# A layer's head in two parts of TensorE, and the experts' rows fetched ahead of a phase border

## What is computed

```python
x = x + _L0_attn_ref(_layernorm(x), ...) + _L0_ffn_ref(...)   # a selective state-space block; FP4 linear layers
x = x + _L1_attn_ref(...) + _L1_ffn_ref(...)                  # gated delta rule; mixture of 8 experts
x = x + _L2_attn_ref(...) + _L2_ffn_ref(...)                  # local attention; gated linear layers
x = x + _L3_attn_ref(...) + _L3_ffn_ref(...)                  # linear attention; gated linear layers
```

```python
uc = silu(conv(u))
dbc = uc @ W_x                       # 256 -> 8 + 16 + 16 columns
dt_r, Bs, Cs = dbc[..., :8], dbc[..., 8:24], dbc[..., 24:]
dt = softplus(dt_r @ W_dt + b_dt)    # 8 -> 256 columns
# then, token by token: h = h * exp(dt * A) + (dt * u) * B;  y = sum over states of h * C
```

## Time and profile before

| what | value |
|---|---|
| median of three runs | 637.83 us (636.1 to 640.2) |
| the profiled execution | 636.67 us, its span 635.0 us |
| TensorE matmul busy | 566.0 us (89%) |
| VectorE busy | 452.7 us (71%) |
| ScalarE busy | 385.8 us (61%) |
| GpSimd busy | 360.9 us (57%) |
| mean granted clock of TensorE | 0.97 of full speed |

### The profile page before, as it was taken

How to read it: one execution, slowest core, us unless ns; L and a number is a source line. 1 busy time by engine, 2 the same in 40 slices (tenths; PEclk the granted TensorE clock), 3 DMA queues, 4 the chain that set the end, 5 groups by cost and what they waited for, 6 DMA issues and landing times. The chain is left out here.

```text
span 635.0 us, 10717 instructions
## 1 busy us (share of the span) xinstructions
PE 566.0 (89%) x3813; PEld 456.0 (72%) x3813; DVE 452.7 (71%) x798; ACT 385.8 (61%) x751; POOL 360.9 (57%) x306
## 2 busy tenths in 40 slices
PE   5999978899999999898887989798999868989997
PEld 2444578799998998576654956798788756776766
DVE  6799798999999986995575797243333575648662
ACT  4679799779979794565459677222211234748670
POOL 0578778988899884688610840864801650224430
PEclk9999699899999999899898999898999999999999
DMA  5035033334434511100350011612412110000002
GB/s 130 4 79 96 13 88 71 84 99 107 112 96 105 100 68 38 39 1 1 88 141 2 2 18 24 160 42 79 131 31 64 39 30 0 1 2 1 2 1 67
DMA packets 43230, 35.77 MB, mean 56 GB/s; under 512 B 11895, under 2 KB 32297, under 8 KB 43178
## 3 DMA queue, kind: packets, MB, share of 16 engines
q1 hardware_dynamic: 42154, 32.99, 21.1%
q0 software_dynamic: 1024, 2.10, 1.1%
HBM read 28.98 MB, written 6.09 MB: 55 GB/s over the span
## 5 line engine op out<-in xcount | busy, mean ns | idle before, releaser
L891 DVE TENSOR_TENSOR_SCAN l0s_ring<-l_XM,l0s_ring,bank 128x512 f32<-128x512 f32 x96 | 114.5, 1259 | 5.3 <-ACT l_XM L602 4.4
L602 ACT ACTIVATE l_XM<-l_DT,l_negA 128x512 f32<-128x512 f32 x120 | 79.7, 712 | 10.2 <-DVE l0s_ring L891 10.0
L749 POOL TENSOR_TENSOR l0s_ring<-l0s_ring,l0s_c_rest 128x1024 f32<-128x1024 f32 x32 | 65.8, 2056 | 18.3 <-DVE l0s_ring L891 9.1
L749 POOL TENSOR_TENSOR l0s_ring<-l0s_ring,all_XF 128x1024 f32<-128x1024 f32 x31 | 66.4, 2146 | 7.9 <-DVE l0s_ring L891 5.5
L449 PE MATMUL bank<-all_ident,l0s_ring 128*128 128x128 f32 x512 | 66.7, 275 | 0.0
L449 PEld LDWEIGHTS bank<-all_ident,l0s_ring 128*128 128x128 f32 x512 | 58.7, 142 | 0.0
L2050 POOL DMA_INDIRECT all_XNT<-gy,all_slot x16 | 15.5, 971 | 37.0 <-DMA gy<-l1s_ys 31.2
L418 PE MATMUL bank<-all_ident,all_XNT 128*128 128x128 f32 x256 | 34.0, 275 | 1.0 <-DVE l0s_ring L891 0.7
L332 PE MATMUL bank<-l_XM,l_wins 128*128 128x512 f32 x64 | 31.8, 642 | 0.9 <-ACT l_XM L546 0.9
L625 ACT ACTIVATE all_XNT<-all_OUTF,l_wins 128x256 f32<-128x256 f32 x72 | 30.5, 495 | 0.2
L418 PEld LDWEIGHTS bank<-all_ident,all_XNT 128*128 128x128 f32 x256 | 29.1, 142 | 2.0 <-DVE l0s_ring L891 0.9
(11 more groups left out here) (452 smaller groups left out, 1594.9 us busy)
## 6 DMA issues: line engine op xcount, KB each, us to landing
l0s_c_rest<-bc_rows SPq DMA_DIRECT2D x16, 512.0 KB, 5.1
all_XF<-bc_rows SPq DMA_DIRECT2D x16, 512.0 KB, 4.9
l_wall<-in_L_ffn_W SPq DMA_DIRECT2D x14, 256.0 KB, 4.6
all_X<-in_L_attn_x SPq DMA_DIRECT2D x4, 256.0 KB, 3.7
gx<-l1m_TD SPq DMA_DIRECT2D x1, 1024.0 KB, 5.2
gy<-l1m_TD SPq DMA_DIRECT2D x1, 1024.0 KB, 8.6
out<-all_X SPq DMA_DIRECT2D x4, 256.0 KB, 3.3
gy<-l1s_ys SPq DMA_DIRECT2D x7, 128.0 KB, 1.8
```

What stands on the lines that cost most here:

```text
L602: nc.scalar.activation(dst, DT[:, j, block_of(n)], ACT.Exp, scale=negA[:, j, n % DS:n % DS + 1]).then_inc(decay_ready, 1)
L749: nc.gpsimd.tensor_tensor(hc[n % CRING][:, :, :], h(n)[:, :, :], wide(c_wide[p % HRING][:, n % 2, :]), ALU.mult).then_inc(hc_ready, 1)
L891: nc.vector.tensor_tensor_scan(h(n)[:, j, :], factor, added, before, ALU.mult, ALU.add).then_inc(h_ready, 1)
```

## The change

**Head of layer 0.** Each block of 512 tokens is cut into two halves of 256, g = 0 and 1. `project` writes half g to partitions 64g to 64g + 39 of bank 4: four matmuls of 256 columns, alternating between the two sets of output columns of the array. `keep_dbc` copies each half by itself, and `DBC` and `wdt` hold half g from partition 64g on. `step_size` is four matmuls of 256 columns with 8 rows each, alternating between rows 0 to 7 and rows 64 to 71 of the array; the first two go to different banks, and the third and fourth each wait until the matmul that wrote their bank before is complete. `spread` is two matmuls of 256 columns, the second waiting for the first; `turn_b` turns the 8 tiles of half 0, waits, and turns those of half 1. `store` is two transfers a block, and `wdt` is loaded twice.

**Layer 1.** `fetch_rows` moves from the head of phase l1s to the end of SP's list in phase l1m; it still waits for the whole scatter. In l1s SP starts with the weights of experts 5 to 7, and `wo` gets a counter of its own. On TensorE, ScalarE and VectorE `experts()` comes first, without the waits for the two chunks, and all 16 chunks follow.

```diff
@@ -154,12 +155,12 @@
         DTU = big.sb("DTU", [P, JT, T])
-        DBC = big.sb("DBC", [DR + 2 * DS, T])
+        DBC = big.sb("DBC", [2 * HALF + DR + 2 * DS - HALF, T // 2])
         win = big.sb("win", [P, 2 * DI])
...
         wx = big.sb("wx", [P, JT, DR + 2 * DS])
-        wdt = big.sb("wdt", [DR, DI])
+        wdt = big.sb("wdt", [HALF + DR, DI])
         wout = big.sb("wout", [P, JT, P])
@@ -256,6 +257,8 @@
             block_of = lambda n: blk(n // DS)
+            half = lambda b, g: slice(b * BLK + g * HBLK, b * BLK + (g + 1) * HBLK)
+            dbc = lambda g, rows, b: DBC[g * HALF:g * HALF + rows, bass.ts(b, HBLK)]
             zy = lambda b, i: ZT[:, (JT * b + i) * BLK:(JT * b + i + 1) * BLK]
@@ -264,13 +267,14 @@
                         sp.wait_ge(dbc_ready, b + 1)
-                        sp.dma_start(bc_rows[:, blk(b)], DBC[DR:DR + 2 * DS, blk(b)]).then_inc(bc_stored[b], 16)
+                        for g in range(2):
+                            sp.dma_start(bc_rows[:, half(b, g)], DBC[g * HALF + DR:g * HALF + DR + 2 * DS, bass.ts(b, HBLK)]).then_inc(bc_stored[b], 16)
 
...
                         if 2 * p % DS == 0:
-                            sp.wait_ge(bc_stored[2 * p // DS], 16)
+                            sp.wait_ge(bc_stored[2 * p // DS], 32)
                         s, at = DS + 2 * p % DS, p % HRING
@@ -289,7 +293,8 @@
                     sp.dma_start(wx[:, :, :], W["L0_attn_W_x"].rearrange("(j p) c -> p j c", p=P)).then_inc(proj_loaded, 16)
-                    sp.dma_start(wdt[:, :], W["L0_attn_W_dt"]).then_inc(proj_loaded, 16)
+                    for g in range(2):
+                        sp.dma_start(wdt[g * HALF:g * HALF + DR, :], W["L0_attn_W_dt"]).then_inc(proj_loaded, 16)
                     sp.wait_ge(zeroed, 2)
@@ -345,19 +350,24 @@
                         pe.wait_ge(u_ready, JT * (b + 1))
-                        pe.wait_ge(proj_loaded, 96)
+                        pe.wait_ge(proj_loaded, 112)
                         if b:
...
                         for j in range(JT):
-                            last = nc.tensor.matmul(S.bank[4][0:DR + 2 * DS, :], wx[:, j, :], UC[:, j, blk(b)], start=(j == 0), stop=(j == JT - 1))
+                            for g in range(2):
+                                last = nc.tensor.matmul(S.bank[4][g * HALF:g * HALF + DR + 2 * DS, 0:HBLK], wx[:, j, :], UC[:, j, half(b, g)],
+                                                        start=(j == 0), stop=(j == JT - 1))
                         last.then_inc(dbc_done, 1)
...
                         pe.wait_ge(dbc_ready, b + 1)
-                        for j in range(JT):
-                            if b:
-                                pe.wait_ge(max_ready, JT * (b - 1) + j + 1)
-                            nc.tensor.matmul(S.bank[6 + j][:, :], wdt[:, j * P:(j + 1) * P], DBC[0:DR, blk(b)], start=True, stop=True).then_inc(dt_done, 1)
+                        if b:
+                            pe.wait_ge(max_ready, JT * b)
+                        for i, (j, g) in enumerate(((0, 0), (1, 1), (0, 1), (1, 0))):
+                            if i >= 2:
+                                pe.wait_ge(dt_done, 2 * JT * b + i - 1)
+                            nc.tensor.matmul(S.bank[6 + j][:, g * HBLK:(g + 1) * HBLK], wdt[g * HALF:g * HALF + DR, j * P:(j + 1) * P], dbc(g, DR, b),
+                                             start=True, stop=True).then_inc(dt_done, 1)
 
@@ -374,20 +384,31 @@
                     def spread(n):
-                        row = S.ident[0:DR + 2 * DS, DR + n % DS:DR + n % DS + 1].broadcast_to([DR + 2 * DS, P])
                         if n == 0:
...
                             pe.wait_ge(dtu_kept, 2 * (n // DS + 1))
-                        nc.tensor.matmul(bank_b[:, :], row, DBC[:, block_of(n)], start=True, stop=True).then_inc(b_spread, 1)
+                        for g in range(2):
+                            if g:
+                                pe.wait_ge(b_spread, 2 * number(n) + 1)
+                            at = g * HALF
+                            row = S.ident[at:at + DR + 2 * DS, at + DR + n % DS:at + DR + n % DS + 1].broadcast_to([DR + 2 * DS, P])
+                            nc.tensor.matmul(bank_b[:, g * HBLK:(g + 1) * HBLK], row, dbc(g, DR + 2 * DS, n // DS), start=True, stop=True).then_inc(b_spread, 1)
 
...
                         pe.wait_ge(w_copied, 3)
-                        for t in range(TILES):
-                            last = nc.tensor.transpose(bank_t[:, t * BC:(t + 1) * BC], DBC[0:BC, bass.ts(t, P)], S.ident[0:BC, 0:BC])
-                        last.then_inc(b_turned, 1)
+                        for g in range(2):
+                            if g:
+                                pe.wait_ge(b_turned, 1)
+                            at = g * HALF
+                            for b in range(NBLK):
+                                for k in range(2):
+                                    t = b * TPB + 2 * g + k
+                                    last = nc.tensor.transpose(bank_t[:, t * BC:(t + 1) * BC], DBC[at:at + BC, b * HBLK + k * P:b * HBLK + (k + 1) * P],
+                                                               S.ident[at:at + BC, at:at + BC])
+                            last.then_inc(b_turned, 1)
 
...
@@ -559,11 +580,13 @@
                         act.wait_ge(dbc_done, b + 1)
-                        nc.scalar.activation(DBC[:, blk(b)], S.bank[4][0:DR + 2 * DS, :], ACT.Copy).then_inc(dbc_ready, 1)
+                        for g in range(2):
+                            last = nc.scalar.activation(dbc(g, DR + 2 * DS, b), S.bank[4][g * HALF:g * HALF + DR + 2 * DS, 0:HBLK], ACT.Copy)
+                        last.then_inc(dbc_ready, 1)
 
...
                         for j in range(JT):
-                            act.wait_ge(dt_done, JT * b + j + 1)
+                            act.wait_ge(dt_done, 2 * JT * b + JT + j + 1)
                             nc.scalar.activation(DTU[:, j, blk(b)], S.bank[6 + j][:, :], ACT.Abs, bias=b_dt[j]).then_inc(abs_ready, 1)
...
@@ -861,7 +884,7 @@
                     def input_of(n):
-                        dve.wait_ge(b_spread, number(n) + 1)
+                        dve.wait_ge(b_spread, 2 * number(n) + 2)
                         if n // DS < 2:
...
@@ -1351,6 +1373,7 @@
                         sp.wait_ge(tt_ready, 32 * NSUB)
+                        fetch_rows(sp, S, E)
 
...
@@ -2021,8 +2044,9 @@
                     def _(sp):
-                        sp.dma_start(wo[:, :], W["L1_attn_Wo"]).then_inc(loaded, 16)
-                        fetch_rows(sp, S, W, E)
+                        for e in range(EARLY + 1, NE):
+                            fetch_expert(sp, W, E, e)
+                        sp.dma_start(wo[:, :], W["L1_attn_Wo"]).then_inc(wo_loaded, 16)
                         for i, n in enumerate("qkv"):
@@ -2172,12 +2196,6 @@
                         def experts():
-                            pe.wait_ge(u_ready, BEFORE)
-                            pe.wait_ge(ut_ready, BEFORE)
-                            pe.wait_ge(st_new, BEFORE)
-                            pe.wait_ge(ss_new, BEFORE - 1)
-                            pe.wait_ge(p_ready, BEFORE)
-                            pe.wait_ge(og_ready, BEFORE)
                             pe.wait_ge(E.rows_loaded, 16 * (2 + SLOTS // P - TILES))
...
@@ -2410,25 +2428,15 @@
 
+                        experts()
                         pe.wait_ge(zeroed, 1)
-                        for c in range(BEFORE):
+                        for c in range(CH):
                             carry(c)
...
                             if c:
-                                outputs(c - 1)
-                        products(BEFORE - 1)
-                        outputs(BEFORE - 1)
-                        experts()
-                        for c in range(BEFORE, CH):
-                            carry(c)
-                            turn_state(c)
-                            if c > BEFORE:
-                                products(c - 1)
-                            states(c)
-                            if c > BEFORE:
                                 outputs(c - 1)
@@ -2770,26 +2776,17 @@
                         nc.vector.tensor_copy(identb[:, :], S.ident[:, :]).then_inc(identb_made, 1)
+                        experts()
                         dve.wait_ge(zeroed, 1)
-                        for c in range(BEFORE):
+                        for c in range(CH):
                             copy_state(c)
                             if c:
-                                products(c - 1)
-                            states(c)
-                            if c:
-                                outputs(c - 1)
-                        products(BEFORE - 1)
-                        outputs(BEFORE - 1)
-                        experts()
-                        for c in range(BEFORE, CH):
-                            copy_state(c)
-                            if c > BEFORE:
```

(6 more changed lines are left out.)

14 lines of the change are left out of this document (7 added, 7 removed).

## The result

The changed kernel takes 633.31 us (median of 22 runs, 630.44 to 638.54), the kernel before 636.15 us (22 runs, 634.13 to 640.37): ratio 0.9958, 95% interval 0.9941 to 0.9975. That is inside the range of the forecast. But the gain is 2.8 us and not 6.3: that the time itself lies only 1.8 us above the forecast's 631.5 is because the kernel before came out 1.7 us faster here than in its three first runs (637.83). The profiled execution took 632.66 us with a span of 630.9 us, against 636.67 and 635.0.

What follows compares the result with a forecast made beforehand. TensorE was taken to bound the head, with VectorE idle before its first input, and the rows' late fetch the border. Head 2.8 plus border 3.5 gave 6.3 us: 637.83 - 6.3 = 631.5 us, range 628.5 to 636.0.

Steps and rivals of the forecast that it cites:

- Projection: Layer 0 head: eight steps of 0.215 us take the time of five, 1.07 us, gaining 0.65 us a block.
- the engine takes records in their order: Projection on TensorE: half 0's second record waits for its first and only runs beside half 1's first; hence five steps.
- The rival of full overlap: Layer 0 head: each pair of matmuls costs half; total gain 7.4 us, 630.4 us; chance 0.14.
- Step sizes: Layer 0 head: both waits for earlier matmuls are covered, all ends at 1.29 us, gaining 0.43 us.
- ScalarE as the bound: Layer 0 head: ScalarE limits two periods to shrinking 1.03 and 0.62 us; fourth keep_dbc 3.4 us earlier, head gives 2.8.
- A start of the scans that is earlier by x brings everything behind it forward by x: From the scans' start to their end VectorE is nearly never idle, so the lead carries on, less first-step losses; 2.8 us.
- a danger of the clock inside the head: Rival: half clock from first step sizes (29 us) to 66 us loses 18 us, giving 650 us; chance 0.06.
- Fetch of the rows: Before phase l1s: SP's longer list is hidden by 1.9 us; the experts' first transpose comes 7.1 to 7.35 us earlier.
- a sign of being wrong: Border before l1s: the prediction is wrong if the rows come more than 1 us behind it.
- The clock at the border: Rival: a half-clock stretch of 3.4 us falls on the experts, half is lost; gain 4.6, 633.2 us; chance 0.16.
- Two chunks at 3.6 us: Behind the experts: two more recurrence chunks cost 2 x 1.79 = 3.6 us, leaving 3.5 us net from the border.
- 3.6 us more room: Gather of results: starts 7.1 us earlier while chunk 8 comes 3.5 us earlier, so it gets 3.6 us more.

Runs made afterwards that it cites:

- the grouped order: Changed kernel with the projection's matmuls ordered half 0 / j 0, half 0 / j 1, half 1 / j 0, half 1 / j 1: one run, 627.63 us.
- the single copy: Changed kernel with one keep_dbc copy of 104 partitions in place of two of 40, W_x padded with zero columns: 629.77 us, ratio 0.9910.
- the delay: Kernel before with the head's edits, plus seven scratch multiplications on VectorE ahead of the first scan input: 642.41 us, ratio 1.0111.
- e_after3: The changed kernel, nothing else altered, run again on the third chip: 626.52 us (6 runs), ratio 0.9888.

## Why the prediction was right or wrong

**Projection: the step that failed is "the engine takes records in their order".** I made five half-steps of it, a gain of 0.65 us. It is four: a gain of 0.86 us a block, and the grouped order shows that the premise was wrong and not only the count. The rival of full overlap was right here.

**Step sizes: right, for another reason.** 1.42 us, a gain of 0.49 where 0.43 was forecast. With full overlap the gain should have been 0.86; the third matmul's wait for the first was called covered, and is not: the second pair starts 0.75 us behind the first (29.33 and 28.58), where two steps take 0.43. The wait costs 0.3 us.

**ScalarE as the bound: right.** It has no idle time in front of the last `keep_dbc`, which is 3.8 us earlier (3.4 forecast), because TensorE's larger gain counts up to the second block. The two copies take 0.77 us, 0.72 forecast. The first input comes 3.3 us earlier (3.0 forecast) and nothing is lost behind it: 3.23 us are there at the end of the scans, where I had 2.8. The way from the first `keep_dbc` to the first input is 41.2 us in all five traces without the head's edits and 37.9 in all six with them (without the single copy and the delay).

**"A start of the scans that is earlier by x brings everything behind it forward by x": failed, for the most part by the granted clock.** Without the head's edits the middle takes 185.98 to 186.71 us in five traces. With them it takes 184.25 to 191.26 us in nine, 187.9 on average, and it goes with its time at the half clock: 10.2 and 13.6 us in the two shortest, 27.2 in the longest. It is not the whole: with 17.0 us of it the middle of `e_after3` takes 187.86 us and that of before 186.32. The mean clock of the head alone was lower in both series, so this is more than one unlucky trace. For the changed kernel it was 0.9673, 0.9681 and 0.9707 in the three sets of runs; the kernel before had 0.9695 beside the second and 0.9708 beside the third, where nothing of the clock was lost. I had looked for a danger of the clock inside the head and at the border, and not in the phases between. Why those phases fall to the half clock more often after a shorter head is open; the one experiment on it missed its size.

**Fetch of the rows: right.** SP ended 2.2 us before ScalarE (1.9 forecast), the border was not held up, and the first transpose stands 7.7 us nearer to it (7.1 to 7.35 forecast). In five of the eight traces with early rows and all chunks behind, the distance from ScalarE's end to it is 1.4 to 1.9 us as here; in the other three the rows land later, and it is 2.6 to 3.2 us. In those three the rows come over 1 us late, which the prediction had named as a sign of being wrong.

**The clock at the border: a rival that holds in some executions.** In four of those eight traces TensorE is at the half clock when the experts begin, for 3.4 us or more, and the experts take 1.4 to 2.9 us longer to the gather (44.09 to 45.58 against 42.67 to 42.80). In the trace of after it is not, since its stretches had come before. The price forecast was 1.7 us.

**Two chunks at 3.6 us: the step that was mis-sized, both ways.** I read the chain as TensorE's own work from the experts on. But the wait for the gather at chunk 8 is the bound there when the chunks are ahead; that the wait is not seen in the trace of before is because the stall behind TensorE's late counters filled the same time. So "3.6 us more room" for the gather was not room but the gain itself. On the chips without the stall the two chunks cost 0.8 us at most and the blocks behind them get some 2 us shorter: the border's edits bring 5.3 us, and the whole change 7.8 (0.9888). On the chips with it the stall comes out of its hole: 18.7 us in place of 13.5, the border's edits bring 0.5 us, and the whole change 2.5 to 2.8. The prediction had named this sign too: the gained time came back as idle engines before chunk 8.

That the time fell inside the range was therefore luck: the head's median gain is close to zero and not 2.8, and the border's 3.5 stands for a gain of 0.5 us on one chip and 5.3 us on another.

## What to carry to other kernels

Where an engine waits for nothing in the trace, look whether another wait ends within a microsecond of the same moment: what stands behind it is covered now and comes out when the first is moved. When two engines stop and start together, look at the third whose counters both wait for, and at when these were raised. The same kernel gained 0.5% on one chip and 1.1% on another, so a change near a gather should be timed on more than one. And a lead of some microseconds early in the kernel is worth only what the clock leaves of it: list the half-clock stretches of both traces before the time that is missing is looked for in the instructions.
